# A transformer block in split precision: four waits moved, and the first feed-forward group prepared inside attention's drain

## The reference

```python
h = _ln(x, g1, be1);  x = _attn(h, h, Wq1, Wk1, Wv1, Wo1, bo1) + x
h = _ln(x, g2, be2);  x = _attn(h, context, Wq2, Wk2, Wv2, Wo2, bo2) + x
h = _ln(x, g3, be3);  y = h @ Wp + bp
a, gate = (y[..., :FF_HID], y[..., FF_HID:])          # FF_HID = 1024
x = a * jax.nn.gelu(gate, approximate=False) @ W2 + b2 + x
```

## Time and profile before

| | us |
|---|---|
| median of 3 runs (3110.99 to 3120.89) | 3120.03 |
| the profiled execution | 3116.79 |
| its span, first to last instruction | 3115.0 |
| PE busy in the span | 2980.8 (96%) |
| DVE / ACT / POOL busy | 2298.5 / 1881.6 / 1423.2 |

### The profile page before, as it was taken

One profiled execution on the slowest core, in us unless ns is written; L12 is line 12 of the kernel. 1 busy time (PEld: TensorE's weight loads), 2 busy tenths in 40 slices (PEclk: granted clock), 3 DMA queues, 4 the chain that ended last, 5 costly groups with the idle time before them and its releaser, 6 DMA issues. The chain is left out here.

```text
span 3115.0 us, 77480 instructions
## 1 busy us (share of the span) xinstructions
PE 2980.8 (96%) x25600; PEld 2592.8 (83%) x25600; DVE 2298.5 (74%) x3846; ACT 1881.6 (60%) x5615; POOL 1423.2 (46%) x978
## 2 busy tenths in 40 slices
PE   7999999999999999899999999999999959999999
PEld 6888888888888888788888888888888848888888
DVE  5777777777777777788888888888888845556554
ACT  6666666666666666667766766776766632332332
POOL 4555555555555554555555555555555530001000
PEclk9999999999999999999999999999999989999999
DMA  7787887887888777788888888888888740001000
GB/s 233 215 240 234 239 239 237 236 241 236 240 237 239 235 233 233 238 246 251 249 246 246 251 247 246 252 248 245 248 247 249 237 115 28 27 27 39 28 27 21
DMA packets 464427, 625.06 MB, mean 201 GB/s; under 512 B 57728, under 2 KB 397056, under 8 KB 464128
## 3 DMA queue, kind: packets, MB, share of 16 engines
q1 hardware_dynamic: 460256, 624.09, 66.9%
q10 hardware_dynamic: 4128, 0.41, 0.1%
HBM read 330.71 MB, written 293.60 MB: 200 GB/s over the span
## 5 line engine op out<-in xcount | busy, mean ns | idle before, releaser
L449 POOL TENSOR_TENSOR at_probs<-at_probs,at_row_inv 128x1024 f32<-128x1024 f32 x512 | 969.7, 1894 | 1125.2 <-DVE at_row_inv L651 1122.2
L498 ACT ACTIVATE at_probs<-at_ps_s,at_neg_max 128x256 f32<-128x256 f32 x2048 | 945.7, 473 | 127.3 <-DVE at_neg_max L624 94.5
L624 DVE TENSOR_REDUCE at_neg_max<-at_ps_s 128x2 f32<-128x512 f32 x1024 | 660.4, 684 | 186.9 <-PE at_ps_s L793 185.2
L643 DVE STREAM_TRANSPOSE at_blocks<-at_probs 128x1024 f32<-128x1024 f32 x512 | 631.0, 1233 | 16.4 <-DMA at_turns<-at_blocks 11.3
L812 PE MATMUL at_ps_o<-at_probs_t,at_v 128*64 128x256 f32 x4096 | 519.8, 389 | 54.0 <-DMA at_probs_t<-at_turns 52.9
L551 ACT ACTIVATE at_qk_hi<-at_ps_qk 128x512 fp32r<-128x512 f32 x512 | 305.4, 596 | 370.3 <-PE at_ps_qk L727 191.1
L812 PEld LDWEIGHTS at_ps_o<-at_probs_t,at_v 128*64 128x64 f32 x4096 | 272.9, 137 | 218.1 <-issue 90.0
L727 PE MATMUL at_ps_qk<-at_h_hi,w_hi 128*128 128x256 f32 x1536 | 431.0, 303 | 13.7 <-ACT at_h_hi L521 8.3
L498 ACT ACTIVATION_READ_ACCUMULATOR at_probs<-at_ps_s,at_neg_max 128x1 f32 x2048 | 415.7, 203 | 0.0
L727 PE MATMUL at_ps_qk<-at_h_hi,w_lo 128*128 128x256 f32 x1536 | 396.9, 281 | 0.0
L727 PEld LDWEIGHTS at_ps_qk<-at_h_hi,w_hi 128*128 128x128 f32 x1536 | 290.9, 189 | 118.8 <-issue 104.3
(11 more groups left out here) (102 smaller groups left out, 6705.6 us busy)
## 6 DMA issues: line engine op xcount, KB each, us to landing
at_turns<-at_blocks SPq DMA_DIRECT2D x2048, 128.0 KB, 3.0
at_probs_t<-at_turns SPq DMA_DIRECT2D x512, 512.0 KB, 4.4
at_xt<-in_x SPq DMA_DIRECT2D x32, 256.0 KB, 6.4
at_xres<-in_x SPq DMA_DIRECT2D x32, 256.0 KB, 2.7
after_self_attention<-at_yout SPq DMA_DIRECT2D x32, 256.0 KB, 2.4
at_xt<-after_self_attention SPq DMA_DIRECT2D x32, 256.0 KB, 6.3
at_xres<-after_self_attention SPq DMA_DIRECT2D x32, 256.0 KB, 2.7
after_cross_attention<-at_yout SPq DMA_DIRECT2D x32, 256.0 KB, 2.4
```

Of the source, the lines that this page charges most:

```text
L449: pool.tensor_tensor(tile, tile, scale, ALU.mult).then_inc(probs_ready, 1)
L498: last = act.activation(probs[:, slot % 2, h, t], scores[:, slot % 2, h, t], ACT.Exp, bias=neg_max[:, slot % 2, i:i + 1], accum_out=row_su ...
L624: nc.vector.tensor_reduce(neg_max[:, slot, r], scores[:, slot, h], AX_X, ALU.max, negate=True).then_inc(neg_max_ready, 1)
L643: nc.vector.transpose(blocks[:, slot].rearrange("p (j a q) -> p a j q", j=QUADS, q=QUAD), probs[:, slot].rearrange("p h t (k j q) -> p (h ...
```

## The change

1. `load_residual` goes from p = 6 to p = 2 of the next sequence, behind that step's stores, with a wait until the last output stored has landed (its sum was made from the rows that the load overwrites). POOL's bias goes from p = 0 to p = 4. The first residual is no longer read at the start.
2. The products with `c_lo` go to the end of the five, and `c_lo` has a semaphore of its own; PE waits for it once a sequence, ahead of the fifth product of the first pair's keys, and for the packed tile ahead of the first.
3. The six constants of attention get two semaphores: ACT waits for the four it needs, POOL for the two biases.
4. The feed-forward weights are read in three transfers of 1 MB, at p = 2, 4 and 6 of the seam.
5. A class `FeedForward` holds the feed-forward's buffers, in part laid over attention's. SP reads the four constants in the seam at p = 0, and group 0 in the drain at p = 0. In the drain DVE takes the statistics at p = 0, normalises at p = 2 and makes `h_lo` at p = 4; POOL makes the power at p = 2; PE transposes at p = 4 into attention's PSUM banks; ACT scales and makes `h_hi` at p = 4. The block behind the barrier starts with the first product.

```diff
     def load(self, sp, i):
+        if i < KT:
+            sp.dma_start(self.raw_wp.rearrange("p (k n) -> p k n", k=KT)[:, i],
+                         self.wp[i * P:(i + 1) * P, :]).then_inc(self.loaded["wp"], 16)
...
+    def load_consts(self, nc, sp):
+            sp.dma_start(self.gamma_c[:], gamma.rearrange("(k p) -> p k", p=P)).then_inc(self.consts_loaded, 16)
+            sp.dma_start(self.beta_c[:], beta.rearrange("(k p) -> p k", p=P)).then_inc(self.consts_loaded, 16)
+            sp.dma_start(self.bp_c[:], bp.rearrange("(k p) -> p k", p=P)).then_inc(self.consts_loaded, 16)
+        sp.dma_start(self.b2_row[:], b2.partition_broadcast(P)).then_inc(self.consts_loaded, 16)
...
+    def transpose_first(self, nc, pe, banks):
+        pe.wait_ge(self.xnorm_ready, 1)
+        for k in range(KT):
+            for t in range(GT):
+                last = nc.tensor.transpose(banks[k][:, t * P:(t + 1) * P], self.xnorm[:, t, k * P:(k + 1) * P],
+                                           self.ident[:])
+        last.then_inc(self.h_transposed, 1)
+
+    def scale_first(self, act, banks):
+        act.wait_ge(self.consts_loaded, 64)
+        act.wait_ge(self.h_transposed, 1)
+        for k in range(KT):
+            last = act.activation(self.h_t[:, k], banks[k][:], ACT.Identity, bias=self.beta_c[:, k:k + 1],
+                                  scale=self.gamma_c[:, k:k + 1])
+        last.then_inc(self.h_t_ready, 1)
+        act.wait_ge(self.h_t_ready, 1)
+        act.activation(self.h_hi[:, 0], self.h_t[:], ACT.Copy).then_inc(self.h_hi_ready, 1)
+
+    def low_first(self, nc, dve):
+        dve.wait_ge(self.h_hi_ready, 1)
+        nc.vector.tensor_tensor(self.h_lo[:, 0], self.h_t[:], self.h_hi[:, 0].bitcast(F32),
+                                ALU.subtract).then_inc(self.h_ready, 1)
...
 # SP, step
-                if part == SEAM and p == 2:
+                if part == SEAM and p >= 2:
                     sp.wait_ge(v_done, PAIRS // 2 * n)
                     sp.wait_ge(qk_done, PAIRS * n)
-                    ff_w.load(sp)
+                    ff_w.load(sp, p // 2 - 1)
                 if part in (LOOP, LAST, SEAM) and p == 6:
                     store(b - 1, stage_behind(part, stage))
-                    sp.wait_ge(y_stored, 16 * b)
-                    load_residual(b, stage)
+                if part == SEAM and p == 0:
+                    ff.load_consts(nc, sp)
+                if part == DRAIN and p == 0:
+                    ff.load_first(sp)
+                if part != FIRST and p == 2:
+                    if counts(c := 16 * (b - 1)):
+                        sp.wait_ge(y_stored, c)
+                    load_residual(b - 1, stage_behind(part, stage))
...
 # POOL, step
-                if part != FIRST and p == 0:
+                if part != FIRST and p == 4:
                     residual(b - 1, stage_behind(part, stage))
+                if part == DRAIN and p == 2:
+                    ff.norm_power(pool, 0)
...
 # ACT
-            act.wait_ge(consts_loaded, 96)
+            act.wait_ge(scales_loaded, 64)
             scale_shift(0, SELF)
...
+                if part == DRAIN and p == 4:
+                    ff.scale_first(act, (ps_qk, ps_misc))
...
 # DVE, step
                 if part == DRAIN and p == 0:
                     ff_w.split_low(nc.vector, 0)
+                    ff.norm_stats(nc, dve, 0, 0)
+                if part == DRAIN and p == 2:
+                    ff.norm_apply(nc, dve, 0, 0)
+                if part == DRAIN and p == 4:
+                    ff.low_first(nc, dve)
...
 # PE
                     yield c_hi[:, 0], hi[:, 0]
-                    yield c_lo[:], hi[:, 0]
                     yield c_hi[:, 0], lo[:, 0]
                     yield c_hi[:, 1], hi[:, 1]
                     yield c_hi[:, 1], lo[:, 1]
+                    yield c_lo[:], hi[:, 0]
...
-                if stage == CROSS:
-                    pe.wait_ge(c_ready, 2 * (b - n + 1))
-                project_pair(ps_qk[:, SEQ:2 * SEQ], p, stage, stage == SELF, "wk").then_inc(qk_done, 1)
+                first = stage == CROSS and p == 0
+                if first:
+                    pe.wait_ge(c_packed_ready, b - n + 1)
+                project_pair(ps_qk[:, SEQ:2 * SEQ], p, stage, stage == SELF, "wk",
+                             c_count=b - n + 1 if first else None).then_inc(qk_done, 1)
...
+                if part == DRAIN and p == 4:
+                    ff.transpose_first(nc, pe, (ps_qk, ps_misc))
```

More of the change, by code:

```diff
@@ L220, in attention @@
+def attention(nc, tag, x_in, ctx_in, x_out, weights, bo, gamma, beta, ff, y_stored):
     n = x_in[SELF].shape[0]
@@ L726, in project_pair @@
                         pe.wait_ge(h_ready, h_count)
+                    if c_count is not None and i == len(passes) - 1:
+                        pe.wait_ge(c_lo_ready, c_count)
                     last = nc.tensor.matmul(out, m[:, p * P:(p + 1) * P], a, start=i == 0, stop=i == len(passes) - 1)
@@ L1021, in _ @@
         def _(act):
[L1022 to L1028 removed]
+            act.wait_ge(f.consts_loaded, 64)
             def step(b, parity, j, part):
```

249 lines of the change are left out of this document (127 added, 122 removed).

## The result

The changed kernel takes 3033.3 us (median of 4 runs, 3032.07 to 3035.1) where the kernel before, run beside it, took 3119.6. The ratio is 0.973, with a 95% interval of 0.9711 to 0.9748.

What follows compares the result with a forecast made beforehand. PE was taken to bound attention, its waits being what can be won. Terms 3.3 + 19 + 12 + 3 + 10 + 1 + 12.8 = 61.1 us took 3116.8 to 3055.7, stated as 3057 us, range 3040 to 3085.

Steps and rivals of the forecast that it cites:

- Where the waits were and what ends them: Attention, p = 0: SP's standstill for the output and the residual's 256 KB make the loads late; 2.5 us for the first.
- The size of a wait: Self attention: 29 waits for turned probabilities, mean 0.7 us, 20.1 in all as upper bound; 19 us taken as gain.
- `c_lo` and cross: Cross attention: 12 of 18.4 us from moving the residual's load, 10 (bounds 0 and 11.6) from moving `c_lo`'s products last.
- Feed-forward behind its first product has nothing changed in it: Feed-forward after its first product: no change, so no term for it in the sum.
- The wait goes with 0.1 us to spare: Cross attention: PE reaches the `c_lo` product at 2039.66 at the earliest, after `c_lo` ends at 2039.53.
- Between the stages: Between self and cross: 3 of 11.2 us from the residual's move, 1 (bounds -5 and 4) from the weights' three transfers.
- The start: Kernel start: ACT no longer waits for the biases before scaling; gain 3.3 us, bounds 0 and 4.5.
- The drain: Drain and feed-forward's start: 17.3 us saved behind the barrier less 4.5 of drain growth, gain 12.8, bounds 7 and 17.3.
- the rival in which DVE and POOL slow each other: Drain: normalising and `h_lo` take twice as long beside POOL's splits; drain grows 11.5 us more, time 3068; chance 0.06.
- The clock: First feed-forward products: a shorter pause may give full clock, up to 2.5 us; left out of the sum, in the range.
- The slower rival: Attention: the residual's load moves the wait to p = 4; 3181 us at 2 us a sequence, 3119 at half; chance 0.05.
- come back elsewhere: Attention: DVE or the load of p = 2 is waited for next; only 19 of 44 us stay, time 3082; chance 0.14.

Runs made afterwards that it cites:

- Part 1 alone: The kernel before with only the residual's load moved behind the stores of p = 2 and POOL's bias at p = 4: 0.9828, 3059.2 against 3111.7 us.
- parts 1 to 4: The kernel before with all of the change but the preparing of group 0 in the drain: 0.9803, 61.3 us faster.
- the second profile: The changed kernel itself, nothing altered, run and profiled again: 0.9747 of the kernel before, 3034.4 us; its profiled span is 3032.6 us.
- the version with group 0 earlier: The changed kernel with group 0 loaded at p = 4 of the last cross sequence and normalised at drain p = 0: 0.973, 3029.3 us.

## Why the prediction fell short, point by point

**Where the waits were and what ends them: right.** The standstill at p = 6 and the transfer made the waits at p = 0; without them none is left in the even parts.

**The size of a wait: wrong, and this is the first step that failed.** I wrote "Gain in self: 0 to 20.1 us; I take 19", with the sum of the idle rows as the upper bound. Part 1 alone gave 25.1 in self and 24.5 in cross. Rows 6 and 8 show why. The eight products ahead of the wait start at 1033.69 in the kernel before, and the next at 1035.66, 1.97 us apart:

```profile
1033.69 1.08 PE L812 MATMUL at_ps_o<-at_probs_t,at_v 128*64 128x256 f32 x8
```

Eight such products take 1.95 - 1.08 = 0.87 us from start to start. PE stood 1.97 - 0.87 = 1.10 us, and the row says 0.89, because the last product's modelled record runs on after the next could have started. The missing 0.21 us in each of 29 waits gives 20.1 + 6.1 = 26.2 in self, against 25.1 measured; the sums over 25 sequences (0.22 us a sequence, above) agree. In cross 18.4 + 6.1 = 24.5 meets the measured 24.5 by luck: there 0.31 us a sequence were hidden, and 0.1 came back elsewhere.

**`c_lo` and cross: the sum right, both terms wrong.** I had 12 for part 1 and 10 for part 2. Part 1 gave 24.5 and part 2 nothing, so that the sum of 22 came near 23.8 is luck. DVE works without a gap from p = 6 to p = 0, and what PE no longer stands for `c_lo` it stands, hidden under the records, for DVE's `o_lo` and `qk_lo`. "The wait goes with 0.1 us to spare" was wrong too: the product comes 0.05 us behind `c_lo`'s end, the distance at which PE follows an operand that it has waited for.

**Self, a further 5.3 us: put at nothing, and the second step that failed.** Part 5 has no term for the even parts, and "Feed-forward behind its first product has nothing changed in it". Yet the kernels with part 5 are faster in both, at the full clock and with no wait gone. In self the 48 products of values in a sequence are recorded with 277 ns on average in the changed kernel and 281 with parts 1 to 4, and start 114.3 ns apart, not 117.7, which is 0.16 us. The projections win another 0.13 and the output's products lose 0.09: together 0.18 to 0.2 us a sequence. In feed-forward, behind the first 200 products, it is 2.9 us (below). Part 5 changes where the tiles lie in SBUF, and that is what I would suspect; no run here separates it, so the cause stays open. Without these 8.2 us the time would have been 3041.5, just inside the range.

**Between the stages: under-sized.** 7.6 us instead of 3 + 1. Part 1 gave 3.0, as forecast; the three pieces 4.2 to 4.7, above the bound of 4, where I expected their new waits to eat most of it.

**The start: right** (3.3; 3.5 in the profile, 2.7 to 3.9 in the others with part 3).

**The drain: near, by two errors.** 14.4 us for 12.8. The chain of group 0 cost more than 4.5: from the last transposes to the barrier it is 78.8 us with parts 1 to 4 (2383.35 to 2462.14) and some 88.7 with part 5, 9.9 more. Of that, 3.6 us are the statistics, as forecast; 3.4 are the last `o_lo`, ready to run when ACT's `o_hi` ended at 2458.86 and held until 2462.28 by `h_lo`. That is the rival in which DVE and POOL slow each other, whose place I had put at POOL's end; POOL was done at 2461.28, and the damage was on DVE. The other 2.9 aren't divided. Part of them is the clock: PE's last twelve products of attention start 0.21 us apart in the changed kernel, at a granted clock of 0.50 (2463.39 to 2465.90), and 0.12 apart with parts 1 to 4. On the other side the kernels with part 1 and without part 5 have a drain that is 4 to 7.5 us shorter (99.1, 98.2 and 95.7 for 103.2), and I had not counted that. Part 5's own share is thus 95.7 - 88.8 = 6.9 us, or 4.6 by the second profile, where the sum had 12.8.

The Trainium skill (SBUF — State Buffer, SBUF: two separate sides) says that the port pair which VectorE and GpSimd share is an exclusive lock for a whole instruction, for an operation of VectorE with two inputs in SBUF against one of GpSimd that reads SBUF, so that the other of the two is blocked and not slowed. The trace agrees for `h_lo`, which has two such inputs: it ends at 2458.30 + 4.06 = 2462.36, 1.08 us behind the end of POOL's splits at 2461.28, and alone it takes 1.22. In the second profile it took 3.69 us and ended 1.09 behind them.

**The clock: left out, worth 1.1 us here.** The granted clock is 0.71 in the 8 us from 2466, in which the first gate product starts, and 1.00 from 2474; the earlier trace rows had 0.57 ahead of that product and 0.69 in the 8 us from it on. PE had been idle for 1.8 us ahead of it and not for most of 17. The first 200 products of feed-forward take 37.4 us in the changed kernel and 38.5 before. Over all runs they take 35.9 to 38.8 us with part 5 and 38.3 to 38.7 without, so in the second profile of the changed kernel (35.9) the clock gave 2.6. The rest of the 4.0 us, 2.9, lies behind those products, where the clock is 1.00 in both kernels: 526.0 us against 528.9 (with part 5 525.7 to 526.2 in all runs, without 527.5 to 528.9). It isn't the clock.

**The rivals.** The waits did not come back elsewhere in self; in cross they did, all of part 2's and some 0.1 us a sequence of part 1's. The slower rival, with the wait moved to p = 4, had 1.0 us of cost a sequence as its point of decision, and the cost was nil.

The sum itself has a slip: 3055.7 and the 3.2 us of the median make 3058.9, not 3057. The error of 22.8 us in the 61.1 is thus: self 11.5 (6.1 of part 1 and 5.3 of part 5, by the table), cross 1.8, between 3.6, drain 1.6, behind 4.0, start 0.2.

## What to carry to other kernels

A sum of idle rows is no upper bound for what a wait costs on PE: compare starts of the same product across a wait, and add what the record of the product before hides. When two waits lie in one loop, remove each alone and both together before adding their prices; the slack of a queue behaves the same way, with two things that each cost next to nothing and together cost a fiftieth of the kernel. And when PE shows 99.9% busy, look at the engine whose row ends 0.05 us before PE's next product starts. And a change that moves no wait there can still shift the even parts by half a per cent, as part 5 did; what in it does so takes a run of its own.

## What the runs showed of the hardware

- Two of DVE's operations stretched beside POOL's splits: four normalisations of 128x256 from 1.37 to 5.27 us, a two-input subtraction of 128x1024 from 1.22 to 4.06. Of the four, the first two took 2.26 and 2.45 us, each ending 0.15 to 0.16 us behind a split, and the others 0.40. POOL paid little: its splits took 4.73 and 6.83 us there, and 4.68 and 6.83 in the version with group 0 earlier, where these operations lie elsewhere.
- A short operation's row can be mostly another engine's time: DVE's two-input subtraction took 0.77 us for 64x8 elements and 1.03 for 64x256, each time ending 0.02 and 0.28 us behind a POOL operation that had started before it; with nothing beside them they took 0.16 and 0.43.
- Without a late transfer the pipeline is periodic to a hundredth: 37.64 us in each sequence of self from sequence 3 on in the changed kernel, 37.82 with parts 1 to 4, where the kernel before lay between 37.97 and 39.41.
